# Raw blocks of the down product split one stage earlier and reloaded as f16 parts, in an adaLN layer with linear attention and a gated feed-forward

## The reference

```
x (2 x 2048 rows, 512 wide), 16 heads; six rows of modulation per batch: sa, ca, ga, sb, cb, gb
h = layernorm(x) * (1 + ca) + sa
x = x + ga * linear_attention(h)            # elu + 1 feature maps, q k v o projections
h = layernorm(x) * (1 + cb) + sb
gate, up, down weights are looked up: w = lut[index], a table of 16 values, 1376 hidden columns
x = x + gb * (silu(h @ gate.T) * (h @ up.T)) @ down.T
```

## Time and profile before

| | |
|---|---|
| median of 3 runs | 1179.18 us (1178.31 to 1180.44) |
| the profiled execution | 1180.3 us, span 1178.5 us |
| TensorE busy (matmuls) | 1115.9 us, 95% of the span |
| VectorE busy | 884.7 us, 75% |
| ScalarE busy | 488.1 us, 41% |
| GpSimd busy | 384.9 us, 33% |
| mean granted TensorE clock | 0.988 of full speed |

### The profile page before, as it was taken

One profiled execution on the slowest core, in us unless ns is written; L12 is line 12 of the kernel. 1 busy time (PEld: TensorE's weight loads), 2 busy tenths in 40 slices (PEclk: granted clock), 3 DMA queues, 4 the chain that ended last, 5 costly groups with the idle time before them and its releaser, 6 DMA issues.

```text
span 1178.5 us, 18789 instructions
## 1 busy us (share of the span) xinstructions
PE 1115.9 (95%) x7508; PEld 613.5 (52%) x7534; DVE 884.7 (75%) x1251; ACT 488.1 (41%) x837; POOL 384.9 (33%) x323
## 2 busy tenths in 40 slices
PE   4899999999999999999999999999999798988887
PEld 2344444454444444445444444444444477777776
DVE  4788978786787787976568777565347699999995
ACT  4678778876654130413113123130313334344442
POOL 1000200003034152525025034250330377776774
PEclk9999999999999999999999999999999899999999
DMA  7930233203204622222113032121311524444551
GB/s 270 330 115 1 86 108 108 72 2 108 73 1 166 239 77 103 77 93 92 52 63 116 35 116 78 71 74 43 116 43 43 170 90 166 160 156 159 168 168 72
DMA packets 72727, 126.07 MB, mean 107 GB/s; under 512 B 5472, under 2 KB 37728, under 8 KB 68544
## 3 DMA queue, kind: packets, MB, share of 16 engines
q1 hardware_dynamic: 72640, 124.88, 31.2%
HBM read 77.15 MB, written 47.71 MB: 106 GB/s over the span
## 4 chain that ended last, share of the span: by engine, by line
PE 75%; DVE 15%; issue 5%; ACT 4%; DMA 1%; POOL 0%; SPq 0%; POOLq 0%; ACTq 0%; DVEq 0%
PE bank L1429 19%; PE bank L1431 19%; PE bank L1430 19%; PE bank L1742 3%; PE bank L1744 3%; PE bank L1743 3%; PE bank L1437 2%; DVE look_buf L1102 1%; DVE qp L1303 1%; PE bank L1581 1%; DVE qp L1301 1%; DMA w_ffn<-in_wmod 1%; DVE w_ffn L1102 1%; DVE hid_f L1274 1%; DVE shared L1338 1%
## 5 line engine op out<-in xcount | busy, mean ns | idle before, releaser
L828 ACT ACTIVATE shared<-bank,sc 128x512 f32<-128x512 f32 (+1 forms) x88 | 60.2, 685 | 387.4 <-PE bank L1431 387.4
L1429 PE MATMUL bank<-h,w_ffn 128*128 128x512 f16 (+1 forms) x528 | 200.4, 380 | 1.8 <-ACT shared L828 1.6
L1430 PE MATMUL bank<-h,w_ffn 128*128 128x512 f16 (+1 forms) x528 | 200.1, 379 | 0.0
L1431 PE MATMUL bank<-h,w_ffn 128*128 128x512 f16 (+1 forms) x528 | 200.1, 379 | 0.0
L1264 DVE SCALAR_TENSOR_TENSOR shared<-bank,sc,shared 128x512 f32<-128x512 f32 (+1 forms) x88 | 65.8, 748 | 137.9 <-issue 69.7
L1429 PE MATMUL bank<-arena,h 128*128 128x512 f16 x256 | 98.5, 385 | 4.2 <-DVE h L1008 1.3
L1430 PE MATMUL bank<-arena,h 128*128 128x512 f16 x256 | 98.5, 385 | 0.0
L1431 PE MATMUL bank<-arena,h 128*128 128x512 f16 x256 | 98.4, 384 | 0.0
L1099 DVE TENSOR_SCALAR look_buf<-look_buf,tab_x,tab 128x512 uint32<-128x512 uint32 x147 | 90.6, 639 | 0.6
L1429 PEld LDWEIGHTS bank<-h,w_ffn 128*128 128x128 f16 (+1 forms) x528 | 52.9, 100 | 68.9 <-issue 11.1
L506 POOL TENSOR_SCALAR sc<-mv 128x4 f32<-128x4 f32 x8 | 2.3, 284 | 254.3 <-DVE mv L1226 254.3
(11 more groups left out here) (293 smaller groups left out, 2708.0 us busy)
## 6 DMA issues: line engine op xcount, KB each, us to landing
hid_dram<-shared SPq DMA_DIRECT2D x80, 256.0 KB, 2.0
w_ffn<-hid_dram SPq DMA_DIRECT2D x16, 1280.0 KB, 6.0
xg<-in_x SPq DMA_DIRECT2D x16, 1024.0 KB, 7.1
qp_dram<-qp SPq DMA_DIRECT2D x8, 1024.0 KB, 4.9
x_dram<-xg SPq DMA_DIRECT2D x8, 1024.0 KB, 3.9
xg<-x_dram SPq DMA_DIRECT2D x8, 1024.0 KB, 8.2
out<-xg SPq DMA_DIRECT2D x7, 1024.0 KB, 5.5
qp<-qp_dram SPq DMA_DIRECT2D x6, 1024.0 KB, 5.3
```

What stands on the lines that cost most here:

```text
L828: act.activation(silu_g[0:m, e % 2], bank[2 + 2 * (e % 2)][0:m], ACT.Silu, scale=c1(C_INV_G)[0:m]).then_inc(silu_g_done, 1)
L1429: pe.matmul(dst, a_hi, b_hi, start=first, stop=False)
L1430: pe.matmul(dst, a_hi, b_lo, start=False, stop=False)
L1431: last = pe.matmul(dst, a_lo, b_hi, start=False, stop=end)
```

## The change

Each chunk of hidden values is split into its two f16 parts in the gate and up stage, where it is made: `hid_full` writes f32 into a ring of two (`hid_f`), ScalarE makes the high half (`hid_hi`), GpSimd the low half (`hid_lo`), both into the ring of three (`hid`), which is f16 now. SyncE stores the parts to `hid_dram` and the f32 values of the ten full chunks to a new `full_dram`. In the down stage `hid_load` brings the parts of A11, A12, A22 and of the tail straight to where TensorE reads them (four transfers a unit), and `full_load` brings the f32 rows, which only the block sums read. The high and low halves of raw blocks and tail go away there. ScalarE still makes the high halves of the sums (`sum_hi`), VectorE their low halves (`sum_lo` moves from GpSimd). The layout of a left block is chunk by chunk now, high beside low. In the last gate and up stage the right sums begin one slot earlier, GpSimd's plane copies are spread over five slots, and the first unit's blocks are loaded and its sums made in slots 6 to 9. The held row `held_u3` has one buffer instead of two, and elsewhere in SBUF.

```diff
-        hid = part(shared, 4 * HID, F32, HIDS, GROUP)
+        hid = part(shared, 4 * HID, F16, HIDS, TILES, 2, P)
...
-        left = [[part(a, at, F16, 2, HALF_K, P) for a, at in home] for home in homes]
+        left = [[part(a, at, F16, HALF_K, 2, P) for a, at in home] for home in homes]
...
+            def full_load(u):
+                g, i, cols = u // 2, u % 2, slice(u % 2 * UNIT, u % 2 * UNIT + UNIT)
+                if i == 0:
+                    for s, count in full_landed(SLOT[(g, FC - 1)]):
+                        sp.wait_ge(s, count)
+                if u >= 2:
+                    sp.wait_ge(left_summed, 4 * (u - 1))
+                sp.dma_start(hid_raw[i], full_dram[g][:, :, cols]).then_inc(full_in[i], 16)
...
                 if u >= 2:
-                    sp.wait_ge(raw_low, 4 * (u - 1))
-                    sp.wait_ge(left_summed, 4 * (u - 1))
-                sp.dma_start(hid_raw[i][:, 0:FC - 1], hid_dram[g][:, 0:FC - 1, cols]).then_inc(hid_in[i], 16)
-                sp.dma_start(hid_raw[i][0:TAIL, FC - 1], hid_dram[g][0:TAIL, FC - 1, cols]).then_inc(hid_in[i], 16)
+                    sp.wait_ge(prod_ready, 7 * (u - 1))
+                for which, k, tile in ((S_A11, 0, t), (S_A12, HALF_K, t), (S_A22, HALF_K, t + 1)):
+                    sp.dma_start(left[i][which], hid_dram[g][:, k:k + HALF_K, tile]).then_inc(hid_in[i], 16)
+                sp.dma_start(left_last[i][0:TAIL], hid_dram[g][0:TAIL, FC - 1, t:t + 2]).then_inc(hid_in[i], 16)
...
-                    elif i == 7:
-                        sp.wait_ge(tf_done, 4 * HALF_K)
+                    elif i == 1:
+                        sp.wait_ge(up_done, SLOT[(GROUPS - 1, 0)] + 1)
+                        hid_load(0)
+                    elif i == 6:
+                        sp.wait_ge(wf_done, 2 * HALF_K)
                         sp.wait_ge(b_planes, 3 * HALF_K + 1)
-                        hid_load(0)
+                        full_load(0)
+                        sp.wait_ge(up_done, SLOT[(GROUPS - 1, 4)] + 1)
                         hid_load(1)
+                        full_load(1)
                     sp.wait_ge(hid_f_done, e + 1)
+                    if j < FC - 1:
+                        sp.dma_start(full_dram[g][:, j], hid_f[:, e % 2]).then_inc(full_out[e % 2], 16)
+                    sp.wait_ge(hid_done, e + 1)
                     sp.dma_start(hid_dram[g][0:m, j], hid[0:m, e % HIDS]).then_inc(hid_out[e % HIDS], 16)
...
+            def hid_lo(e, j):
+                m = rows_of(j)
+                pool.wait_ge(hid_hi_done, e + 1)
+                whole = hid_f[0:m, e % 2].rearrange("p (t n) -> p t n", t=TILES)
+                pool.tensor_tensor(hid[0:m, e % HIDS, :, 1], whole, hid[0:m, e % HIDS, :, 0], ALU.subtract).then_inc(hid_done, 1)
...
+            def hid_hi(e, j):
+                m = rows_of(j)
+                act.wait_ge(hid_f_done, e + 1)
+                if e >= HIDS:
+                    act.wait_ge(hid_out[e % HIDS], 16 * (e // HIDS))
+                whole = hid_f[0:m, e % 2].rearrange("p (t n) -> p t n", t=TILES)
+                act.activation(hid[0:m, e % HIDS, :, 0], whole, ACT.Copy).then_inc(hid_hi_done, 1)
...
                     silu_gate(SLOT[(g, j)], j)
                     if n < GROUPS:
                         run(before, i)
+                    hid_hi(SLOT[(g, j)], j)
                     if n < GROUPS:
                         run(after, i)
...
-                if more:
-                    left_hi(u + 1, S_A11)
                 hold(u, 0)
                 if more:
-                    left_hi(u + 1, S_S1)
+                    sum_hi(u + 1, 0)
                 hold(u, 1)
                 if more:
-                    left_hi(u + 1, S_S2)
-                    left_hi(u + 1, S_A12)
+                    sum_hi(u + 1, 2)
+                    sum_hi(u + 1, 1)
                 hold(u, 2)
                 if more:
-                    for which in (S_S3, S_S4, S_A22):
-                        left_hi(u + 1, which)
-                    last_hi(u + 1)
+                    sum_hi(u + 1, 3)
...
-                if e >= HIDS:
-                    dve.wait_ge(hid_out[e % HIDS], 16 * (e // HIDS))
-                dve.scalar_tensor_tensor(hid[0:m, e % HIDS], bank[3 + 2 * i][0:m], c1(C_HID)[0:m], silu_g[0:m, i],
+                if e >= 2:
+                    dve.wait_ge(hid_done, e - 1)
+                    count = dict(full_landed(e - 2))[full_out[i]]
+                    if count:
+                        dve.wait_ge(full_out[i], count)
+                dve.scalar_tensor_tensor(hid_f[0:m, i], bank[3 + 2 * i][0:m], c1(C_HID)[0:m], silu_g[0:m, i],
...
-                dve.wait_ge(hid_in[u % 2], 32 * (u // 2 + 1))
+                dve.wait_ge(full_in[u % 2], 16 * (u // 2 + 1))
...
+            def sum_lo(u, i):
+
+                dve.wait_ge(sum_high, 4 * u + (0, 2, 1, 3)[i] + 1)
+                block = left[u % 2][S_S1 + i]
+                dve.tensor_tensor(block[:, :, 1], left_sum[i], block[:, :, 0], ALU.subtract).then_inc(sum_low, 1)
...
+                if i == 8:
+                    left_sums(0)
+                if i == 9:
+                    for k in (0, 2, 1, 3):
+                        sum_lo(0, k)
...
-                if u + 1 < DOWN_UNITS:
-                    left_part(u + 1, 0)
+                if more:
+                    left_sums(u + 1)
+                    sum_lo(u + 1, 0)
+                    sum_lo(u + 1, 2)
                 left_u3(u)
-                if u + 1 < DOWN_UNITS:
-                    left_part(u + 1, 1)
+                if more:
+                    sum_lo(u + 1, 1)
+                    sum_lo(u + 1, 3)
                 out_row(u, 0)
                 out_scale(u, 0)
...
-                pe.wait_ge(raw_low, 4 * u + 1)
+                pe.wait_ge(hid_in[i], 64 * (u // 2 + 1))
                 product(0, x_left, True)
```

More of the change, by code:

```diff
@@ L208, in adaln_kernel @@
         wt_last = part(arena, 6 * wt_words, F16, 2, HID)
-        w_full, t_full = hid_f, h_f[:, :, :].rearrange("p a (b n) -> p (a b) n", b=2)
-        hid_raw = [part(w_ffn, GU * GROUP + i * FC * UNIT, F32, FC, UNIT) for i in range(2)]
+        w_full, t_full = qn_f, h_f[:, :, :].rearrange("p a (b n) -> p (a b) n", b=2)
+        hid_raw = [part(w_ffn, GU * GROUP + i * (FC - 1) * UNIT, F32, FC - 1, UNIT) for i in range(2)]
         qp_flat = qp[:, :, :].rearrange("p a b -> p (a b)")
@@ L251, in adaln_kernel @@
         x1_dram = nc.dram_tensor("x1_dram", (GROUPS, P, TILES * HID), F32, kind="Internal").ap()
[L252 removed]
+        hid_dram = nc.dram_tensor("hid_dram", (GROUPS, P, FC, TILES, 2, P), F16, kind="Internal").ap()
+        full_dram = nc.dram_tensor("full_dram", (GROUPS, P, FC - 1, GROUP), F32, kind="Internal").ap()
         def sems(names):
@@ L318, in landed, with full_landed @@
             return [(hid_out[k], 16 * ((e - k) // HIDS + 1)) for k in range(HIDS) if e >= k]
+        def full_landed(e):
+            past = [i for i, (g, j) in enumerate(gj for stage in STAGES for gj in stage) if i <= e and j < FC - 1]
+            return [(full_out[k], 16 * sum(i % 2 == k for i in past)) for k in range(2)]
         def wait_apart(eng, s, n):
@@ L1402, in _ @@
                         {i: [lambda i=i: right_step(i)] for i in range(FC)} if s == GROUPS - 1 else {})
-            left_part(0, 0)
-            left_part(0, 1)
             for u in range(DOWN_UNITS):
+                more = u + 1 < DOWN_UNITS
                 if u:
@@ L1739, in product @@
                     l, r = left[i][PRODUCTS[k][0]], wt[PRODUCTS[k][1]]
+                    order = {S_S1: 1, S_S3: 2, S_S2: 3, S_S4: 4}
+                    if PRODUCTS[k][0] in order:
+                        pe.wait_ge(sum_low, 4 * u + order[PRODUCTS[k][0]])
                     for jj in range(HALF_K):
                         end = jj == HALF_K - 1 and not rest
-                        pe.matmul(dst, l[:, 0, jj], r[:, jj, 0], start=start and jj == 0, stop=False, skip_group_check=True)
-                        pe.matmul(dst, l[:, 0, jj], r[:, jj, 1], start=False, stop=False, skip_group_check=True)
-                        last = pe.matmul(dst, l[:, 1, jj], r[:, jj, 0], start=False, stop=end, skip_group_check=True)
+                        pe.matmul(dst, l[:, jj, 0], r[:, jj, 0], start=start and jj == 0, stop=False, skip_group_check=True)
+                        pe.matmul(dst, l[:, jj, 0], r[:, jj, 1], start=False, stop=False, skip_group_check=True)
+                        last = pe.matmul(dst, l[:, jj, 1], r[:, jj, 0], start=False, stop=end, skip_group_check=True)
                     for to, tile, cols in rest:
-                        a = slice(tile * P, tile * P + P)
-                        pe.matmul(to, rows[:, 0, a], last_w[:, 0, cols], start=False, stop=False, skip_group_check=True)
-                        pe.matmul(to, rows[:, 0, a], last_w[:, 1, cols], start=False, stop=False, skip_group_check=True)
```

(4 more changed lines are left out.)

111 lines of the change are left out of this document (34 added, 77 removed).

## The result

Four runs after the change took 1170.99 us in the median (1167.90 to 1171.33), four of the kernel before 1179.51 (1178.31 to 1180.44): a ratio of 0.9922, 95% interval 0.9903 to 0.9942. The kernel is faster by 8.5 us, 0.8%. The forecast was 1165, range 1145 to 1180. The profiled execution after took 1171.33 us, its span 1169.5.

What follows compares the result with a forecast made beforehand. VectorE was taken to bound the down stage, where TensorE had gaps. From the profiled 1180.3 us, 1180.3 - 41.7 + 13.7 + 8 + 4 + 2 = 1166.3, so 1165 as a median, range 1145 to 1180.

Steps and rivals of the forecast that it cites:

- -41.7, the down stage: Down stage: VectorE's unit falls below 12.78 us, TensorE becomes the bound and its waits go, gaining 41.7 us.
- Rival E: Down stage: VectorE stays the bound because strided f16 outputs cost as much as the company did; 1185, chance 8%.
- only its company changes: Down stage: VectorE's operation count stays; without GpSimd's low halves beside it, its second sum takes 0.73 us, not 1.82.
- 640-element operations near 0.73: Down stage, sign of being right: VectorE's operations of 640 elements last near 0.73 us.
- +13.7, the first gate and up stage: Third hid_full waits for the first store behind the x load; output projection 11.2 us later, lower clock 2.5 us more.
- +8, the last gate and up stage: GpSimd's copies and low halves slow VectorE's loop around the right sums: 8 us lost, bounds 0 and 14.
- the upper bound of 14: Last gate and up stage: TensorE stalls 14 us if VectorE loses all of GpSimd's time in the loop.
- +4, the seam: Reloads ahead of slot 6's store delay hid_full of slot 8: 4 us, bounds 0 and 7 (the old seam wait).
- +2, transfers: Down stage: 3.44 MB a unit asks for 269 GB/s and fits with little room; 2 us, bounds 0 and 40.
- Rival C: Down stage: transfers bound it, every unit waiting for its f32 copy; at 225 GB/s the kernel takes 1204; chance 15%.
- Rival D: Lookup stages: VectorE overfull with low halves, at most 5 us in each of two stages; 1166 to 1177, chance 12%.
- Rival B: Gate and up stages: their costs hide, as the store lands before VectorE asks; 1140 to 1150, chance 20%.

Runs made afterwards that it cites:

- with the seam clear: Changed kernel with the second f32 reload put in front of slot 8's stores and the second f16 reload in front of slot 9's: 1162.4 us.
- the cheap one: Kernel before with one part of the change alone, VectorE making the low halves of the block sums: 1154.1 us.
- the dear one: Splitting the raw blocks early; run as the changed kernel with GpSimd making the sums' low halves again: 1177.3 us.
- the moved transfers: Changed kernel with the x load behind the first three slots' stores: 1162.7 us; with the owT load and x1 store behind first stores too: 1156.7 us.
- the four edits: Changed kernel with first stores ahead of the transfers, weight copies a stage earlier, silu ahead of the high halves and reloads spread: 1139.0 us.

## Why the prediction was right, and where it was off

The sum named 1166.3 for a profiled execution; it was 1171.3. Term by term:

**-41.7, the down stage.** Right, and exactly that: with the seam clear it is 252.0 - 210.3. TensorE became the bound, at 12.76 us a unit. Rival E is refuted: the strided f16 outputs took 817 ns a low half, as the contiguous ones of the kernel before with `sum_lo` on VectorE did (817). A low half in the kernel after (990 to 1140) and in that other kernel (990 to 1120):

```profile
L1325 DVE TENSOR_TENSOR w_ffn<-qp,w_ffn 128x640 f16<-128x640 f32 x18 | 14.2, 817 | 0.0
```

```profile
L1306 DVE TENSOR_TENSOR w_ffn<-qp,w_ffn 128x640 f16<-128x640 f32 x15 | 11.8, 817 | 0.0
```

That VectorE gains nothing in count and only its company changes holds as well: 130 operations in 150 us at 15.18 a unit are 13.2 a unit, 153 at 12.76 are 13.0, and their busy time fell from 14.1 us a unit to 10.3. But the row that I gave for it is another one. The second sum of 1.82 stood beside GpSimd's row addition and not beside its low halves, and it takes 1.9 still. The low halves' price was in other rows, such as the third sum's 2.01 against 0.81. The sum was not harmed, as it had the row additions as a term of their own (9.6 to 12.6). For the same reason the sign "640-element operations near 0.73" came true only in part: they last 0.82, and the second sum 1.9. What I left out is a price for each of the two parts, and so I didn't see that the cheap one is worth 25.5 and the dear one 8.7 more, or 16.2 with the seam clear (226.5 - 210.3).

**+13.7, the first gate and up stage.** Mechanism right, measured 15.6. The hole is 12.30 - 1.11 = 11.2, as said. I had named only the 1 MB of x ahead of the store; the moved transfers show that owT and x1 in the queue weigh more (7.4 against 5.8). The half clock cost 12 matmuls at 0.43 instead of 0.215, 2.6 (2.5 said). Not foreseen: a wait of 1.4 for GpSimd's next layer norm, which the kernel before doesn't have. The other 0.4 stay open.

**+8, the last gate and up stage.** Measured 8.1, but by luck: two errors cancel. I had put 2.95 us of GpSimd's work into a slot and two thirds of it lost, 2.0; there are 4.1 us (a copy beside VectorE takes 0.94, not 0.585) and 1.89 are lost, under a half.

The Trainium skill (SBUF — State Buffer, "SBUF: two separate sides") says that the loser of the shared port stands still for the whole instruction of the other. I had taken the upper bound of 14 from it. The loss here is smaller than that, and GpSimd's copies grew by 1.1 us a slot besides: both engines lose a part, as they would if they took turns, instruction by instruction, which would still agree with the page. My step from it to the upper bound was too long, as it had GpSimd win every turn; that they took turns is argued from the durations, and no run here shows it apart.

**+4, the seam.** Under-sized: 7.2, just above the old seam wait that I had given as its upper bound. The wait of `hid_full` for a store behind the reloads was named; I took the middle of the bounds, though 3.7 MB at 322 GB/s in front of that store were already 11 us in the text, and I left out the lower clock level behind the waits (1.6).

**+2, transfers.** Nothing, by 271 against 326 GB/s. Rival C is refuted for this change. Its mechanism is there at 4.42 MB a unit, and not yet at 3.77.

**Rival D** (VectorE overfull in the lookup stages) is refuted: from the fifth `hid_full` of the third stage to the first of the last one it is 347.97 us before (525.41 to 873.38) and 347.95 after (542.60 to 890.55). **Rival B** is refuted for the change itself, as the hole of 12.30 us was there; it is the case that the four edits bring about: it had 1140 to 1150, and 1139.0 was measured.

The 5.0 us between sum and measurement are then 1.6 of start-up, 1.9, 0.1, 3.2 less 2, and 0.2 that stay open.

## What to carry to other kernels

When a change has two parts that relieve the same engine, price each alone: here the part without side costs was worth three quarters of the gain, and the other became worth its costs only once transfers, copies and silu had been moved. A shorter ring can turn every transfer ahead of its store in the queue into a wait of the engine that fills it, so look for what stands in front of the store in program order, not for its usual landing time. A loop shortened ahead of an unrelated wait gives part of its gain to that wait; fix both before judging either.

## What the runs showed of the hardware that was not expected

- The same three f16 reloads took 3.97 us to issue on SyncE right behind the issue of 1.3 MB (the row at 934.34), and 1.51 at 1036.33 in the down stage, where SyncE had issued nothing for 9.6 us. What is issued behind them is late for this alone. That the filled queue holds the issue up is likely, but no run shows it apart.
- TensorE's clock falls within the hole: over 384 to 385, with TensorE idle since 380, the granted clock is 0.64, over 385 to 390 it is 0.50, the 1.2 GHz level, and it is back at 1.00 (2.4 GHz) over 398 to 399, after 12 matmuls. Behind the hole of 1.80 us it had not fallen.
- The same code up to the first `hid_full` took 360.0 to 363.3 us in the profiles of this study.
